# Projection stage: rotary features as even and odd chunks, the split into bfloat16 parts shared with GpSimd, parts stored by head

## The reference

```python
cos, sin = _cos_sin(s, d_model)                      # (1024, 128) each
ct_q  = x @ Wd_q_w + Wd_q_b                          # 256 -> 128, "latent"
query = heads(ct_q @ Wu_q_w + Wu_q_b) + heads(_rope(ct_q @ Wq_r_w + Wq_r_b, cos, sin))
ct_kv = x @ Wd_kv_w + Wd_kv_b
key   = heads(ct_kv @ Wu_k_w + Wu_k_b) + heads(_rope(x @ Wk_r_w + Wk_r_b, cos, sin))
value = heads(ct_kv @ Wu_v_w + Wu_v_b)
# _rope: x0, x1 = even and odd features; out = (x0*cos - x1*sin, x1*cos + x0*sin), interleaved
# 16 heads of 16 features; x is layer-normalised first
```

## Time and profile before

| | us |
|---|---|
| median of three runs | 2306.32 (2297.45 to 2309.36) |
| the profiled execution: time | 2311.8 |
| the profiled execution: span | 2309.9 |
| projection stage, to attention's first product | 244.8 |
| busy over the span: PE / DVE / ACT / POOL | 2057.3 / 1719.7 / 1117.1 / 630.2 |

### The profile page before, as it was taken

The page is one execution under the profiler, slowest core; times in us unless marked ns, Lnnn a source line. Parts: engine busy times, 40 slices in busy tenths (PEclk is TensorE's granted clock), DMA queues, the critical chain, the costliest instruction groups (busy, mean ns, idle before and its releaser), DMA issues. The chain is left out here.

```text
span 2309.9 us, 26254 instructions
## 1 busy us (share of the span) xinstructions
PE 2057.3 (89%) x7010; PEld 766.3 (33%) x7010; DVE 1719.7 (74%) x2510; ACT 1117.1 (48%) x1448; POOL 630.2 (27%) x408
## 2 busy tenths in 40 slices
PE   7889699999999999987899989788878887789997
PEld 3444133232332322312344433233333332234443
DVE  4788899898998989922355565998989898935554
ACT  3444066666666666660232335665567556212221
POOL 0000200000000000000000006998989898900000
PEclk9999599999999999997899998999999999799999
DMA  3223324222332224112200003343434344310000
GB/s 106 87 81 82 56 38 65 39 43 43 51 52 43 38 43 56 20 36 70 77 0 0 0 0 112 100 111 109 115 99 116 102 110 108 93 38 13 15 18 27
DMA packets 98900, 139.44 MB, mean 60 GB/s; under 512 B 12880, under 2 KB 52128, under 8 KB 98784
## 3 DMA queue, kind: packets, MB, share of 16 engines
q1 hardware_dynamic: 98784, 138.00, 26.1%
HBM read 111.62 MB, written 25.95 MB: 60 GB/s over the span
## 5 line engine op out<-in xcount | busy, mean ns | idle before, releaser
L739 DVE TENSOR_REDUCE mx<-max_bank 128x1 f32<-128x512 f32 x960 | 618.0, 687 | 56.9 <-PE max_bank L637 56.5
L727 ACT ACTIVATE probs<-score_bank 128x1024 f32<-128x1024 f32 x512 | 496.6, 1021 | 292.2 <-PE score_bank L651 291.3
L1449 PE MATMUL ys_bank<-outs,rec_diag 128*128 128x512 f32 x512 | 281.7, 678 | 119.3 <-POOL outs L1385 107.6
L637 PE MATMUL max_bank<-ks,qs 96*128 96x512 bf16 x960 | 333.5, 387 | 0.0
L651 PE MATMUL score_bank<-qs,ks 99*128 99x512 bf16 x1024 | 310.8, 385 | 13.6 <-issue 12.3
L1377 POOL TENSOR_TENSOR ring<-u,bc 128x1024 f32<-128x1024 f32 x128 | 300.8, 2357 | 13.7 <-ACT u L1571 13.7
L1385 POOL TENSOR_TENSOR outs<-ring,bc 128x1024 f32<-128x1024 f32 x112 | 263.5, 2354 | 57.1 <-DVE ring L1784 57.1
L694 PE MATMUL o_bank<-probs,vg 128*32 128x512 f32 x2048 | 272.7, 605 | 0.5 <-ACT probs L727 0.5
L1203 DVE SCALAR_TENSOR_TENSOR hid_f<-hid_bank_f,relu_f 128x512 f32<-128x512 f32 x128 | 87.0, 689 | 224.9 <-ACT relu_f L1175 223.8
L1622 ACT ACTIVATE a_bank<-dt,decay_s 128x512 f32<-128x512 f32 x256 | 171.2, 685 | 165.5 <-DVE ring L1784 153.3
L1125 PE MATMUL hid_bank_f<-xn_f,wfc_f 128*128 (+1 forms) x512 | 240.5, 603 | 10.4 <-DVEq L1194 5.2
(11 more groups left out here) (188 smaller groups left out, 2048.0 us busy)
## 6 DMA issues: line engine op xcount, KB each, us to landing
bc<-bc_scr SPq DMA_DIRECT2D x128, 512.0 KB, 4.9
qk_parts<-parts SPq DMA_DIRECT2D x32, 384.0 KB, 2.8
ks<-qk_parts SPq DMA_DIRECT2D x96, 128.0 KB, 4.8
qs<-qk_parts SPq DMA_DIRECT2D x192, 64.0 KB, 4.9
o_scr<-o_sb SPq DMA_DIRECT2D x32, 256.0 KB, 2.0
xin<-in_x_dram SPq DMA_DIRECT2D x8, 512.0 KB, 4.5
o_in<-o_scr SPq DMA_DIRECT2D x16, 256.0 KB
out_dram<-x_out_f SPq DMA_DIRECT2D x8, 512.0 KB, 3.0
```

Of the source, the lines that this page charges most:

```text
L637: nc.tensor.matmul(max_bank[(r + a) % MB][:], qs[r][0:SROWS, half, j, qt * P:(qt + 1) * P], ks[r][0:SROWS, j, kh * TW:(kh + 1) * TW], star ...
L727: nc.scalar.activation(probs[:, s % 2, 2 * pair:2 * pair + 2], score_bank[pair][:], ACT.Exp, scale=SOFTMAX_SCALE).then_inc(probs_ready, 1)
L739: nc.vector.tensor_reduce(mx[:, a // HU, a % HU:a % HU + 1], max_bank[(r + a) % MB][:], AX_X, ALU.max)\
L1449: mm = nc.tensor.matmul(y_bank[f][:], rec_diag[:, f * NS + n], outs[:, g % OUTS, f], start=(n == 0), stop=(n == NS - 1))
```

## The change

Weights, biases and tables are laid out so that chunk 0 of a rotary product holds the even features (x0) and chunk 1 the odd ones (x1), for all 16 heads; the products with swapped weights go, and both chunks use one cos and one sin table. Units fall from 16 to 12, in another order. VectorE's `rotate` now does a side (k, then q) with both chunks: four products with the tables, two additions of the compact product written into the PSUM bank, and one subtraction and one addition. GpSimd does `leave_rest` and `low`. `finish` works in the PSUM bank of the variance and stands behind both rotations. ScalarE loads one table set at the start. The parts are stored by group of four heads, 32 partitions to a DMA, and neighbouring parts are loaded by one DMA. The loops over tiles are written out.

```diff
+def runs_of(parts): ...            # neighbouring equal steps of a part list become one run
+Q_RUNS, K_RUNS = runs_of(Q_PARTS), runs_of(K_PARTS)      # 5 and 3 runs
+STACK_LOAD = 16 * (len(K_RUNS) + 2 * len(Q_RUNS))
-        UNITS = 16
+        UNITS = 12
@@ sync
+            for t in range(NT):
...
+                for u in range(CHUNKS):
+                    sp.wait_ge(low_kept, t * CHUNKS + u + 1)
+                    side, c = 1 - u // DC, u % DC
+                    for n in range(NG):
+                        sp.dma_start(split_scr[(side * B + b) * NG + n, :, c * (HD // 2):(c + 1) * (HD // 2), :,
+                                               half * TW:(half + 1) * TW].rearrange("s i j t -> (i j) s t"),
+                                     parts[n * (P // NG):(n + 1) * (P // NG), u]).then_inc(parts_out[u], 16)
@@ gpsimd
+            def leave_rest(t, u):
...
+                nc.gpsimd.tensor_tensor(rest[:, u], full[:, u], parts[:, u, 0], ALU.subtract).then_inc(rest_ready, 1)
+            def low(t, u):
+                pool.wait_ge(mid_kept, t * CHUNKS + u + 1)
+                nc.gpsimd.tensor_tensor(parts[:, u, 2], rest[:, u], parts[:, u, 1], ALU.subtract).then_inc(low_kept, 1)
+            for t in range(NT):
+                for side in range(SIDES):
+                    leave_rest(t, 2 * side)
+                    leave_rest(t, 2 * side + 1)
+                    low(t, 2 * side)
+                    low(t, 2 * side + 1)
@@ tensor
+            for t in range(NT):
+                more = t + 1 < NT
                 pe.wait_ge(normed, t * DC + DC)
+                latent(t, 0)
+                latent(t, 1)
+                if more:
+                    turn(t + 1)
+                rotary(t, 1, 0)
+                rotary(t, 1, 1)
+                if more:
+                    mean(t + 1)
+                compact(t, 1, 0)
+                compact(t, 1, 1)
+                rotary(t, 0, 0)
+                rotary(t, 0, 1)
+                if more:
+                    var(t + 1)
+                compact(t, 0, 0)
+                compact(t, 0, 1)
+                values(t, 0)
+                values(t, 1)
@@ scalar
+            nc.scalar.preload_act_table_set("natural_log_exp_and_others")
...
                 high(t, 0)
-                if with_next:
-                    guess(*following(b, half))
                 high(t, 1)
+                if more:
+                    guess(t + 1)
                 middle(t, 0)
+                middle(t, 1)
                 high(t, 2)
-                middle(t, 1)
                 high(t, 3)
                 middle(t, 2)
                 middle(t, 3)
@@ vector
             def finish(t):
                 dve.wait_ge(rs_guess, t * 2 + 2)
+                nc.vector.scalar_tensor_tensor(var_bank[:], var_bank[:], EPS, guess_rs[:], ALU.add, ALU.mult)
...
+            def rotate(t, side):
...
+                for c, tables in enumerate(((cos, sin), (sin, cos))):
+                    dve.wait_ge(proj_ready, first + c + 1)
+                    for i, table in enumerate(tables):
+                        nc.vector.scalar_tensor_tensor(r[:, 2 * c + i], proj[2 + c][:], bias[:, c:c + 1], table,
+                                                       ALU.add, ALU.mult).then_inc(rotated, 1)
+                for c in range(DC):
+                    dve.wait_ge(proj_ready, first + 3 + c)
+                    dve.wait_ge(rotated, n + (1 if c == 0 else 4))
+                    nc.vector.scalar_tensor_tensor(proj[c][:], proj[c][:], bias[:, 2 + c:3 + c], r[:, 3 * c], ALU.add, ALU.add)\
+                        .then_inc(rotated, 1)
+                for c in range(DC):
...
+                    nc.vector.tensor_tensor(full[:, u], proj[c][:], r[:, 2 - c], ALU.subtract if c == 0 else ALU.add)\
+                        .then_inc(summed, 1)
+            for t in range(NT):
+                more = t + 1 < NT
+                rotate(t, 1)
+                if more:
+                    centre(t + 1)
+                rotate(t, 0)
+                if more:
+                    finish(t + 1)
+                keep_v(t, 0)
+                keep_v(t, 1)
@@ load_stack
-    for n in range(len(Q_PARTS)):
-        rows = slice(n * HD, (n + 1) * HD)
-        eng.dma_start(k[rows], k_in[:, :, K_PARTS[n], :]).then_inc(done, 16)
+    for row, part, n in K_RUNS:
+        eng.dma_start(k[row * HD:(row + n) * HD], k_in[part * HD:(part + n) * HD]).then_inc(done, 16)
+    for row, part, n in Q_RUNS:
         for h in range(2):
...
@@ program
-    qk_parts = nc.dram_tensor("qk_parts", (B * 2 * DC, P, 3, S), BF16, kind="Internal").ap()
+    qk_parts = nc.dram_tensor("qk_parts", (2 * B * NG, 3, HD, G, S), BF16, kind="Internal").ap()
```

More of the change, by code:

```diff
@@ L38, with runs_of @@
 MROWS = SROWS + 3
-STACK_LOAD = 16 * 3 * len(Q_PARTS)
+CHUNKS = 2 * DC
+def runs_of(parts):
+    found = []
+    for row, part in enumerate(parts):
+        if found and found[-1][1] + found[-1][2] == part:
+            found[-1][2] += 1
+        else:
+            found.append([row, part, 1])
+    return found
+Q_RUNS, K_RUNS = runs_of(Q_PARTS), runs_of(K_PARTS)
+STACK_LOAD = 16 * (len(K_RUNS) + 2 * len(Q_RUNS))
 LIF_STEPS, BETA, THRESHOLD = 5, 0.9, 1.0
@@ L287, in tile @@
-            def tile(b, half, with_next):
-                t = b * 2 + half
-                pe.wait_ge(normed, t * DC + DC)
[L290 to L297, removed]
@@ L299, in _, with latent, rotary @@
-            turn(0, 0)
-            mean(0, 0)
-            var(0, 0)
-            pe.wait_ge(consts_in, CONSTS)
-            tiles(pe, tile)
+            def latent(t, u):
+                if t:
+                    pe.wait_ge(summed, (t - 1) * CHUNKS + DC + u + 1)
+                for k in range(DC):
+                    mm = nc.tensor.matmul(proj[u][:], (wdq, wdkv)[u][:, k], xn[:, t % 2, k], start=(k == 0), stop=(k == DC - 1))
+                mm.then_inc(proj_ready, 1)
+            def rotary(t, side, c):
+                bank = proj[2 + c]
+                if side == 1:
+                    if t:
+                        pe.wait_ge(v_kept, (t - 1) * 2 + c + 1)
+                else:
+                    pe.wait_ge(rotated, t * SIDES * ROTS + 2 * c + 2)
+                cols = slice(c * P, (c + 1) * P)
+                if side == 1:
+                    for k in range(DC):
+                        mm = nc.tensor.matmul(bank[:], wkr[:, k, cols], xn[:, t % 2, k], start=(k == 0), stop=(k == DC - 1))
+                else:
+                    mm = nc.tensor.matmul(bank[:], wq[:, 1, cols], ct[:, 0], start=True, stop=True)
+                mm.then_inc(proj_ready, 1)
@@ new lines, in values @@
+            def values(t, pair):
+                pe.wait_ge(rotated, t * SIDES * ROTS + ROTS + 2 * pair + 2)
+                for j in range(2):
+                    tok = slice((2 * pair + j) * P, (2 * pair + j + 1) * P)
+                    mm = nc.tensor.matmul(proj[2 + pair][:, j * D:(j + 1) * D], ct[:, 1, tok], wv[:], start=True, stop=True)
+                mm.then_inc(proj_ready, 1)
+            turn(0)
+            mean(0)
+            var(0)
+            pe.wait_ge(consts_in, CONSTS)
+            for t in range(NT):
+                more = t + 1 < NT
+                pe.wait_ge(normed, t * DC + DC)
+                latent(t, 0)
[16 more added lines that the diff above has]
+                values(t, 1)
@@ L342, in middle @@
                 nc.scalar.activation(parts[:, u, 1], rest[:, u], ACT.Copy).then_inc(mid_kept, 1)
-            def tile(b, half, with_next):
-                t = b * 2 + half
+            keep_x(0)
+            square(0)
+            guess(0)
+            act.wait_ge(consts_in, CONSTS)
+            for t in range(NT):
+                more = t + 1 < NT
                 for u in range(2):
@@ L363, in tile, with centre @@
                 middle(t, 3)
-            keep_x(0, 0)
-            square(0, 0)
-            guess(0, 0)
-            act.wait_ge(consts_in, CONSTS)
-            tiles(act, tile)
         @block.vector
         def _(dve):
-            nc.vector.sem_inc(centred, DC)
-            nc.vector.sem_inc(rs_step, 1)
-            nc.vector.sem_inc(rotated, 2)
-            nc.vector.sem_inc(v_kept, 2)
-            nc.vector.sem_inc(summed, 2)
-            nc.vector.sem_inc(low_kept, CHUNKS)
-            def centre(b, half):
-                t = b * 2 + half
+            def centre(t):
@@ L423, in leave_rest @@
[L423 to L436 removed]
+                    nc.vector.tensor_tensor(xn[:, t % 2, c], xc[:, c], var_bank[:], ALU.mult).then_inc(normed, 1)
@@ L1866, in lay_out @@
     a = {k: np.asarray(x) for k, x in v.items()}
[L1868 to L1869 removed]
+    even = np.arange(D).reshape(NG, G, HD // 2, 2)[..., 0].transpose(0, 2, 1).reshape(P)
+    rows = np.concatenate([even, even + 1])
     def cols(w):
```

274 lines of the change are left out of this document (99 added, 175 removed).

## The result

The changed kernel takes 2312.05 us (median of 14 runs, 2305.63 to 2317.06), the kernel before on the same chip 2302.93 (14 runs, 2294.24 to 2309.36): ratio 1.0042, 95% interval 1.0027 to 1.0057. It is slower by 0.4%: the interval leaves out 1, and the difference is under the 0.5% that the prediction counts as a change one can tell. I had forecast 2303, a gain of 3.7 us. A second comparison gave 1.0002 (0.9979 to 1.0025). The two intervals don't overlap, and it is the kernel before that moved more: its mean is 2302.1 in the first job (several kernels measured together on one chip) and 2306.0 to 2308.9 in the four later ones, that of the changed kernel 2311.7 and 2308.9. So jobs differ by more than the interval of one job allows for.

What follows compares the result with a forecast made beforehand. It took the projection stage to be paced by the order of waits, no engine being full. Start -2.6, seven tiles +4.5 and tail -5.6 gave -3.7 us, forecast 2303 us; range for 8 in 10, 2282 to 2316.

Steps and rivals of the forecast that it cites:

- the clock: TensorE's two pauses per projection tile drop its clock to half: 1.5 us for the long, 0.9 for the short.
- the long pause: TensorE idle 4.0 us between a tile's last value product and the next tile's start; always charged 1.5 us.
- the sign: Whole kernel forecast 3.7 us faster; a clock cost 0.5 us a tile above the charge would make it slower.
- What bounds the kernel: Projection stage: no engine is full; the order of waits between VectorE, ScalarE and TensorE sets 27.3 us a tile.
- VectorE's and TensorE's load: Per projection tile, VectorE loses eight subtractions, 4.8 us; TensorE loses six products, 5.2 us.
- the new loop: A steady projection tile, laid along the new order, takes 24.8 us at full clock, 2.5 below the old one.
- rival B: Projection stage's clock holds, or pauses come out shorter: tiles of 24.8 us, whole kernel 2286 us; chance 0.27.
- rival C: Slow stretches behind projection pauses cost twice the charge: tiles of 29.6 us, whole kernel 2321 us; chance 0.13.
- Table loads: One preloaded ScalarE table set removes two loads from the start-up path, 2.6 us; nothing in the steady loop.
- GpSimd: Eight subtractions per projection tile at 1.25 us each, 10 us a tile, costing nothing in the loop.
- The tail: From the last tile's xn to attention's first product: 29.1 us against 34.7, 5.6 less, with GpSimd on the path.
- Stores: 128 stores of the parts for 32, some 7 us of issues a tile on SP, all hidden.

Runs made afterwards that it cites:

- e_fill: Changed kernel with useless products in both TensorE pauses of a tile, two ahead of the variance, four behind the values: 2288.89 us, 0.9913 of the kernel before.
- p_fill_short: Projection stage alone of the changed kernel, two useless products in the short pause and none in the long one: 251.03 us.
- p_after: Projection stage alone of the changed kernel, everything behind it left out: 255.88 us, against 257.89 for the same cut of the kernel before.
- a_again: The changed kernel run once more, unaltered, beside the kernel before on the same chip: 2309.26 us, ratio 1.0002.
- p_tables: Projection stage alone of the kernel before, with only the one table set preloaded: 254.68 us, against 257.89 without the preload.
- f_loads: Whole changed kernel with attention's stack loads issued part by part again, 18 DMAs a group where it has 13: 2312.92 us.
- cut pair: Projection stage alone, everything behind it left out, of the kernel before and of the changed kernel: 257.89 and 255.88 us.
- pa_: Projection stage and attention only, of the kernel before and of the changed kernel: 1052.62 and 1052.60 us.
- f_preload: Whole kernel before with only the one ScalarE table set preloaded: 2304.14 us, ratio 0.9989 to the kernel before.
- r_: Attention left out, its output filled with the values, in the kernel before and in the changed kernel: 1534.19 and 1539.07 us.
- e_order: Changed kernel with centre and finish moved ahead of the additions, latents in the transposes' banks, and middle and turn moved: 2253.51 us, ratio 0.9752.

## Why the prediction was wrong

Two steps failed. The first is a term of the sum: the clock, charged with 2.4 us a tile, cost 3.2 (15.0 + 7.1 us in seven tiles), because the slow stretch behind the long pause outlasts the one group of four that I charged. It made the seven tiles 3 us longer than forecast; the stage by itself is still shorter, by 2.0 to 2.9 us for 3.7. The second step is unspoken: that what the stage gains arrives at the end. That is where the sign turned, in part by a low draw of the kernel before, and for the rest its cause stays open.

*What bounds the kernel, VectorE's and TensorE's load, the new loop*: right. The loop at full clock is 24.47 (e_fill; forecast 24.8), its two stretches 14.7 and 9.8 (14.85 and 9.95). The waits are the two named, a little shorter than laid out (3.71 for 4.0, 2.17 for 2.5). `finish` in PSUM takes 0.70 an operation.

*The clock*: right as a mechanism, against rival B, and the first term that was mis-sized. I charged 1.5 for the long pause and 0.9 for the short, 2.4 a tile. The long one costs 2.1 (p_fill_short's profile; 2.5 by whole runs), because the slow stretch outlasts the group of four whose length I had read in the earlier trace rows; "the matmul behind them a little" came to up to a microsecond. With both left, the seven tiles take 195.8 (first profile), 192.8 (p_after) and 191.7 (a_again), mean 193.4; that is 7.1 more than with the short one filled, so beside long pauses the short one costs 1.0 a tile (0.7 by whole runs), nearly as forecast, and 0.6 without them. Sum: 171.3 at full clock, 15.0 and 7.1, against the forecast's 173.6, 10.5 and 6.3 (190.4). The Trainium skill, "TensorE: Matmul & The Clock Gate", section "Why this matters for your kernels", warns of idle gaps between bursts of matmuls that are longer than the short pauses here. Its warning holds for the long ones: all 14 behind the first tile in the two profiles of the changed kernel were followed by a slow group, though of seven in p_fill_short one was not. The section says nothing of pauses like the short ones; of those, 11 of 14 were followed by a slow group here, and three of seven with the long pause filled.

This is rival C's mechanism at a third of its extra price: C charged 4.8 a tile, 2.4 more than I did, and it came to 0.8 more, (15.0 + 7.1 - 16.8) / 7. The sign turns from 0.5 us a tile more, I wrote; with 0.3 back for the shorter loop the tiles stayed just under that, and the stage alone did stay shorter.

*Table loads*: -2.6 at the start forecast. p_tables gains 3.2, of which 1.2 before T of tile 0; the loads had also cost the old loop 0.24 us a tile. T of tile 0 came 2.15, 4.1 and 2.9 us earlier than before's in the first profile, a_again and f_loads, and 1.3 in the cut pair: the term is right in size, and single executions scatter by as much. *GpSimd*: 1.16 us an operation, 1.25 by the line through the earlier trace rows. ScalarE's `middle` waited for it, 8.1 us in all in the stretch shown, but neither VectorE nor TensorE. The Trainium skill, "GPSIMD Engine Reference", section "Performance versus the Vector engine", gives 1.96 times VectorE for rows of 2048 elements, 1.35 us by my estimate for the 512 here; measured is 1.16 / 0.69 = 1.7, and the measurement decides. *The tail*: 29.1 forecast, 29.2 measured (217.82 to 247.03), 28.0 in a_again; the working has a slip of 0.2, since 12.9 + 10.0 is 22.9 and not 23.1. *Stores*: hidden; none of the waits in the stretch shown ends with a store.

*The sum*: the stage ends 2.2 us later (first profile), 5.1 and 1.0 earlier (a_again, f_loads); cut off alone it is 2.0 shorter. Forecast 3.7 shorter, so 1 to 2 us of the miss lie in the stage, in the clock term. The whole kernel is 3.3 us slower by the pooled means, some 5 us from where the stage alone would put it; by a_again alone it would be 2 to 4, by the first job 11 to 12. That the sign came out against me is thus in part a low draw of the kernel before in the first job.

*What stays open*: those 5 us. For attention (pa_), the stack loads (f_loads) and the table set (f_preload) the runs show no loss, but each pair could hide 2 to 5 us; what follows attention (r_) could hide all of it. The profiles don't show them either: from attention's first product to the end of the span before takes 2065.1, after 2061.6, a_again 2064.3, f_loads 2068.1, e_fill 2067.1, e_order 2064.7, and only f_preload less, 2054.4. The before runs reach such low draws (16 of the 73 lie under 2300, none of after's 26), and without those 16 their mean is 2309.8, after's within a microsecond or so. f_loads has none in 12 either, f_preload 3 in 12. That the kernels with the changed stage draw them less often is an observation; why, no run tells. The intervals also leave room for less than 5, and for nothing.

## What to carry to other kernels

Work taken from an engine that waits gains little until the chain is in order: here what VectorE must finish before TensorE's next burst. With that order the change gained 55 us, without it nothing that the whole kernel shows. Price a TensorE pause by everything that runs slowly behind it, the next units too, and test it with useless matmuls in the pause. Compare stages cut off alone where a gain of a few us is at stake; the stage's runs lay within 5 us, those of the whole kernel before within 25.

## What was not expected of the hardware

TensorE finished earlier by doing more: with e_fill's useless products the whole kernel took 2288.9 us, without them 2310. The same attention took 784.8 and 789.9 us in two executions. A pause of 1.52 us left the clock alone in e_order; of 14 pauses of 2.2 us in the two profiles of the changed kernel 11 were followed by a slow group (2.40 to 3.65 us), and with the other pause filled 3 of 7. A pause of 3.71 us was not always followed by one either (p_fill_short, 47.11). A store of 96 KB from 32 partitions landed in 1.9 us, one of 384 KB from 128 had taken 2.8.
